# A graph-attention and a graph-mean layer, fused: straight code for the batches, features ahead of scores, and adjacency words transposed by DMA

## What is computed

```python
feats = einsum('bnf,hfu->bhnu', x, W)                   # layer 0, 8 heads
dense = leaky_relu(e_self[..., :, None] + e_neigh[..., None, :], 0.2)
dense = dense + NEG_BIG * (1.0 - adj[:, None])
out = einsum('bhij,bhju->bhiu', softmax(dense), feats) + b
x = layernorm(x + relu(out))
agg = einsum('bij,bjf->bif', adj, x) / maximum(sum(adj, -1), EPS)   # layer 1
x = layernorm(x + relu(concatenate([x, agg], 2) @ W1.T))
```

## Time and profile before

| | us |
|---|---|
| median of 3 runs | 3521.29 |
| lowest and highest run | 3521.27, 3525.59 |
| the profiled execution's own time | 3527.3 |
| its span, first to last instruction | 3525.3 |
| TensorE (PE) busy | 3383.6, 96% |
| VectorE (DVE) busy | 2466.5, 70% |
| ScalarE (ACT) busy | 1870.4, 53% |
| GpSimd (POOL) busy | 284.8, 8% |

### The profile page before, as it was taken

The page is one execution under the profiler, slowest core; times in us unless marked ns, Lnnn a source line. Parts: engine busy times, 40 slices in busy tenths (PEclk is TensorE's granted clock), DMA queues, the critical chain, the costliest instruction groups (busy, mean ns, idle before and its releaser), DMA issues.

```text
span 3525.3 us, 135227 instructions
## 1 busy us (share of the span) xinstructions
PE 3383.6 (96%) x58432; PEld 2881.7 (82%) x58432; DVE 2466.5 (70%) x4364; ACT 1870.4 (53%) x2457; POOL 284.8 (8%) x252
## 2 busy tenths in 40 slices
PE   5999999999999999999999999999999999999998
PEld 4978879787796878969789697887978879788795
DVE  4857668576685766858578585784857758577685
ACT  3736546365464645646456373563746547355463
POOL 0020200202001020010201002010020200202001
PEclk9999999999999999999999999999999999999999
DMA  4113131131321213112031221312213121131210
GB/s 170 52 43 117 39 103 56 50 99 38 103 64 55 93 35 106 64 54 93 29 113 57 67 81 32 117 50 81 68 37 119 43 97 52 44 116 39 85 34 25
DMA packets 98401, 248.46 MB, mean 70 GB/s; under 512 B 14720, under 2 KB 14720, under 8 KB 97792
## 3 DMA queue, kind: packets, MB, share of 16 engines
q1 hardware_dynamic: 97792, 239.38, 20.5%
HBM read 205.26 MB, written 34.08 MB: 68 GB/s over the span
## 4 chain that ended last, share of the span: by engine, by line
PE 85%; DVE 8%; issue 5%; ACT 1%; DMA 0%; SPq 0%; DVEq 0%; ACTq 0%; POOL 0%; POOLq 0%
PE six L887 70%; PE pair L887 10%; DVE xs L766 2%; DVE stats L771 2%; PE six L1023 2%; DVE feat L658 1%; PE pair L916 1%; PE six L916 1%; PE pair L924 1%; PE six L924 1%; DVE rs L779 0%; ACT x_parts L502 0%; DVE trl L647 0%; DVE nb L781 0%; DVE x_parts L636 0%
## 5 line engine op out<-in xcount | busy, mean ns | idle before, releaser
L887 PE MATMUL six<-rest,mask 128*128 128x65 bf16 x16384 | 1549.8, 195 | 4.2 <-issue 4.0
L887 PE MATMUL six<-x_parts,mask 128*128 128x65 bf16 x16384 | 1549.4, 192 | 1.9 <-issue 1.3
L887 PE MATMUL six<-third,mask 128*128 128x65 bf16 x16384 | 1549.3, 192 | 0.2
L887 PEld LDWEIGHTS six<-x_parts,mask 128*128 128x128 fp8e4 x16384 | 1536.0, 97 | 8.9 <-issue 7.6
L887 PEld LDWEIGHTS six<-third,mask 128*128 128x128 fp8e4 x16384 | 1536.6, 98 | 0.0
L887 PEld LDWEIGHTS six<-rest,mask 128*128 128x128 fp8e4 x16384 | 1530.7, 96 | 6.9 <-issue 5.6
L479 ACT ACTIVATE step<-s_bc,n_step 128x1024 uint16<-128x1024 f32 x1024 | 1093.5, 1137 | 382.1 <-DVE mask L716 381.8
L716 DVE TENSOR_TENSOR mask<-adj_t,step 128x1024 uint16<-128x1024 uint16 x1024 | 651.3, 685 | 22.6 <-ACT step L479 22.6
L887 PE MATMUL six<-adj_t,x_parts 128*128 128x512 fp8e4 x1536 | 388.1, 380 | 7.1 <-ACT x_parts L502 5.6
L422 POOL TENSOR_TENSOR s_bc<-feat,rden 128x512 f32<-128x512 f32 x112 | 123.9, 1111 | 2998.0 <-DVE s_bc L759 2969.2
L887 PEld LDWEIGHTS six<-adj_t,x_parts 128*128 128x128 f16 x1536 | 146.4, 98 | 184.8 <-issue 23.6
(11 more groups left out here) (124 smaller groups left out, 4954.1 us busy)
## 6 DMA issues: line engine op xcount, KB each, us to landing
s_bc<-self_scores SPq DMA_DIRECT2D x128, 512.0 KB, 3.7
adj_nat<-in_adj_dram SPq DMA_DIRECT2D x96, 512.0 KB, 3.8
xs<-in_x_dram SPq DMA_DIRECT2D x128, 256.0 KB, 2.8
out_dram<-mask SPq DMA_DIRECT2D x128, 256.0 KB, 3.3
adj_nat<-in_x_dram SPq DMA_DIRECT2D x64, 256.0 KB, 5.0
step<-in_x_dram SPq DMA_DIRECT2D x64, 256.0 KB, 3.6
mask<-in_adj_dram SPq DMA_DIRECT2D x32, 512.0 KB, 5.0
xs<-in_L_gnn_W_dram SPq DMA_DIRECT2D x1, 2048.0 KB, 11.2
```

The costliest lines, as they stand in the source:

```text
L887: return pe.matmul(o, l, r, start=start, stop=stop, skip_group_check=True)
```

## The change

- No engine has a loop over batches: `Fori` gives way to a Python loop, and 16 batches are written out (TensorE has some 55,000 rows of program in place of 7,000). The `stand` increments go.
- A batch begins with the features of tile 4, then the scores; the features of tile 5 are made in three pieces, around the transposes of the score rows and the maximum. The waits for the old batch's last sum now stand at the start of the new one, ahead of the first product that writes where this sum reads; `x_low(7)` is ahead of this sum on VectorE. The second scores have PSUM bank 5, the maximum bank 3.
- ScalarE's copy with the row sum writes an adjacency word (`adj_word`, three slots, scaled by EDGE; the sums are scaled with it, and `degc` takes this back). SP transposes each word into `adj_t` by `dma_start_transpose` (`turn_adj` on SP). TensorE's `turn_adj` and VectorE's `adj_rows` go.
- The order of loads and of the words changes: adjacency tiles 2 and 3 are the staged ones of the first round; tiles 4 to 7 are loaded when the word of the tile four earlier is made.
- `turn_x1(0)` stands after key tile 2, not 1.
- The value rows are computed as before.

```diff
+            def adj_words(b, t):
+                landed = a_in[t % 4]
+                act.wait_ge(landed.sem, landed.at(b, 16 * (t // 4 + 1)))
+                if t >= WORD_SLOTS:
+                    turned = adj_turned[t % WORD_SLOTS]
+                    act.wait_ge(turned.sem, turned.at(b, 16 * (t // WORD_SLOTS)))
+                act.activation(adj_word[:, t % WORD_SLOTS], adj_rows_at(t), ACT.Copy, scale=float(EDGE),
                                accum_out=deg_sum[:, t:t + 1]).then_inc(deg_row.sem, 1)
...
+            def turn_adj(b, t):
+                sp.wait_ge(deg_row.sem, deg_row.at(b, t + 1))
+                sp.dma_start_transpose(adj_t[:, :, col(t)],
+                                       adj_word[:, t % WORD_SLOTS, :]).then_inc(adj_turned[t % WORD_SLOTS].sem, 16)
...
                 for t in range(T):
-                    for late in {4: (3, 4), 5: (5,)}.get(t, ()):
-                        load_late_adj(b + 1, late)
+                    if t == 1:
+                        sp.wait_ge(agg_ps.sem, agg_ps.at(b, 2 * KC))
+                    for turned in {1: (0, 1), 2: (2,), 5: (3, 4), 6: (5,), 7: (6,)}.get(t, ()):
+                        turn_adj(b + 1, turned)
+                    for late in {0: (4,), 1: (5,), 2: (6,), 5: (7,)}.get(t, ()):
+                        load_adj(b + 1, late)
                     sp.wait_ge(res_ok.sem, res_ok.at(b, t + 1))
                     load_x(b + 1, t)
                     if t >= 2:
                         store_y(b, t - 2)
                 store_y(b, T - 2)
+                turn_adj(b + 1, T - 1)
                 store_y(b, T - 1)
...
-                dve.wait_ge(at_sb.sem, at_sb.at(b, T))
+                all_turned(dve, b)
...
             def batch(b, more):
 
-                pe.wait_ge(sc_f32.sem, sc_f32.at(b, 1))
-                scores(b, 1)
-                features(b, 4)
+                if b >= 1:
+                    pe.wait_ge(o_sum.sem, o_sum.at(b - 1, T - 1))
+                features(b, 4)
+                pe.wait_ge(ft_sb.sem, ft_sb.at(b, HALF))
+                scores(b, 1)
+                if b >= 1:
+                    pe.wait_ge(o_sum.sem, o_sum.at(b - 1, T))
+                    pe.wait_ge(o2_sb.sem, o2_sb.at(b - 1, T))
+                pe.wait_ge(sc_f32.sem, sc_f32.at(b, 1))
+                features(b, 5, range(0, 2))
                 pe.wait_ge(sc_f32.sem, sc_f32.at(b, 2))
...
-            with pe.Fori(0, B - 1) as b:
-                batch(b, True)
-            batch(B - 1, False)
+            for b in range(B):
+                batch(b, b + 1 < B)
```

More of the change, by code:

```diff
@@ L201, in gat_sage_kernel @@
         tail_in = [Signal(sem(f"tail_in{t}"), 16) for t in range(HALF)]
[L202 to L207, removed]
+        a_in = [Signal(sem(f"a_in{s}"), 32) for s in range(4)]
         y_stored = [sem(f"y_stored{s}") for s in range(2)]
@@ L216, in gat_sage_kernel, with all_turned @@
         xt_lo = signal("xt_lo", T)
-        at_ps = signal("at_ps", T)
-        at_sb = signal("at_sb", T)
+        adj_turned = [signal(f"adj_turned{s}", 16 * len(range(s, T, WORD_SLOTS))) for s in range(WORD_SLOTS)]
+        def all_turned(engine, b):
+            for turned in adj_turned:
+                engine.wait_ge(turned.sem, turned.at(b, turned.per_batch))
         ft_ps = signal("ft_ps", T)
@@ L281, in col @@
             return slice(c * P, (c + 1) * P)
[L283 to L288, removed]
+        N_CONST = 6
         block = ctx.enter_context(nc.Block())
@@ L382, in _ @@
                 sp.wait_ge(sums_ps.sem, sums_ps.at(b, H * GROUPS))
-                stand(sp)
-                for t in range(STAGED, T):
+                for t in (2, 3):
                     load_adj(b + 1, t)
@@ L561, in batch @@
                         act.wait_ge(rdeg_ok.sem, rdeg_ok.at(b, 1))
[L562 to L564 removed]
+                        all_turned(act, b)
+                    for row in WORDS_AT.get(t, ()) if more else ():
+                        adj_words(b + 1, row)
                 ln1_root(T - 1)
@@ L572, in _ @@
                 x_high(0, t)
-            for t in DEG_ORDER:
-                degrees(0, t)
-            with act.Fori(0, B - 1) as b:
-                batch(b, True)
-            batch(B - 1, False)
+            for t in range(T):
+                adj_words(0, t)
+            for b in range(B):
+                batch(b, b + 1 < B)
         @block.vector
@@ L877, in _ @@
                 x_low(0, t)
-            for t in range(T):
-                adj_rows(0, t)
-            with dve.Fori(0, B - 1) as b:
-                batch(b, True)
-            batch(B - 1, False)
+            for b in range(B):
+                batch(b, b + 1 < B)
         @block.tensor
@@ L1102, in _ @@
                 turn_x(0, t)
-            for t in range(T):
-                turn_adj(0, t)
-            with pe.Fori(0, B - 1) as b:
-                batch(b, True)
-            batch(B - 1, False)
+            for b in range(B):
+                batch(b, b + 1 < B)
 _INS = ["x", "adj", "L0_gnn_W", "L0_gnn_b", "L0_gnn_a_self", "L0_gnn_a_neigh", "L1_gnn_W"]
```

134 lines of the change are left out of this document (41 added, 93 removed).

## The result

The changed kernel takes **3372.4 us** (median of 4 runs, 3370.7 to 3374.4) against 3521.6 us for the kernel before on the same chip. The ratio is 0.9574, with a 95% interval from 0.9557 to 0.9591: 149 us less, 4.3%. The forecast was 3368 us in a range from 3340 to 3430. The profiled execution took 3371.0 us, with a span of 3369.2, against 3527.3, the one that the prediction's sum was made against: 156.3 us less, where the sum had 153.2.

What follows compares the result with a forecast made beforehand. TensorE's work and gaps were taken as the bound. Per batch, 6.9 us at the boundary, 2.7 from transposes and 0.7 from a wait give 10.3; 14 times this, 7.0 and 2 leave 3374.1, less 6.0: 3368 us, range 3340 to 3430.

Steps and rivals of the forecast that it cites:

- What bounded the kernel: Whole kernel: TensorE is busy 3383.6 us, 96% of the span, so its work and its few gaps, 142 us, count.
- The boundary: From a batch's last `neighbours(7)` product to the next batch's first word in the heads: 22.9 us falls to 16.0.
- The transposes: DMA transpose of an adjacency word on SP's queue: taken as 5 us to land, between 2.8 or 3.7 and 7.6.
- the packet bound: Upper limit for one DMA transpose: 64 runs of 256 bytes per engine at 118 ns a packet, 7.6 us.
- Transposes off TensorE: Tail of a batch: six adjacency transposes among the products, in three pairs of 0.45 + 0.45 us, leave TensorE: 2.7 us.
- `turn_x1(0)`: Moved one key tile later, its products cover TensorE's wait for the features' evacuation: 0.7 us a batch.
- The start: Batch 0, words and transposes through three slots: rows at about 81, 2 us of gain counted.
- (1): Overlapping DMA transposes of 6 to 10 us delay the first mask: 3417 us at 8 us each; chance 0.15.
- (2): DMA transposes run one behind another, making the kernel slower than before: about 3770 us at 10 us each; chance 0.08.
- (3): The "issue" gap at batch boundaries stays in straight code, 3 to 4 us less gained each: about 3420 us; chance 0.10.
- (4): ScalarE, waiting at words 6 and 7 for transposes, stalls TensorE, from some 9 us a transpose; chance 0.05 with the unknown.
- a late first mask: Sign that the forecast is wrong: VectorE's first mask in the heads waiting for a DMA; no size given.

## Why the prediction was right, step by step

**What bounded the kernel.** Right. TensorE's work and its few gaps were all of it, and 40 us of transposes put back cost 40 us. What the prediction left open is how the gap's two costs hang together. It took stall, tail chain and low clock as one lump, 22.9 - 16.0 us, and set the new order against it. The lump was right and its parts were not asked for: straight code alone returns stall and clock, 65 to 76 us, and the order has 22 us to give in this kernel. Together that is 87 to 98 us beside the 100 of the sum (14 x 6.9 + 3.6), and with the transposes' 40 and the wait's 12 it comes to 139 to 150 us beside the 149 measured. The order could give more, 48 us, but once TensorE's part is shorter, SP's chain ends last.

**The boundary: 16.0 us forecast, 15.8 measured in the mean of 15.** It was 22.9 before, so 7.1 us were gained, where the sum had 6.9. At the boundary shown, of 16.3 us, by its own steps, with 0 at 1102.27: store issued at 3.1 (3.3 forecast) and landed 3.2 later; `y_out(7)` done at 6.9 (7.2); score store issued at 7.3 (7.6) and landed at 10.2, 2.9 us later, the longest of the 15 (their median is 2.1 us, and the forecast had 2.3, to 9.9); broadcast 4.1 (3.7); step 1.16 (1.06); mask 0.69. TensorE's own work in it was sized at 14.5 us; it is busy 15.23. The period between boundaries is (3164.49 - 1102.27) / 10 = 206.2 us, against a forecast of 206.4.

The last row of a later boundary, from which the period is counted:

```profile
3161.74 2.75 PE six L856 x12
```

One loss was not in the forecast: behind the first word TensorE waits again, 0.7 us in the window shown, since VectorE makes masks, value parts and evacuations at that place with 98% of its time. It is part of the 16.6 us above, of which it is about half.

**The transposes: 5 us forecast, 3.3 measured** as the median of all. That of word 7, on which the term rests, has a median of 4.2 us over the 15 boundaries, and the eight of the crowded start have one of 4.4. The value taken lay between the rows for plain transfers and the packet bound, and so did the result. The greatest landing was 5.9 us, under the bound of 7.6. That bound's premise, runs of 256 bytes, holds (1056 packets for 256 KB); the mean time of a packet, which it used, was too long for them: by the difference of the two pages, (27.1% x 3369 - 20.5% x 3525) x 16 / 135,168, a packet of theirs took an estimated 23 ns, not 118. What the prediction did not price is the issue: 1.25 us of SP for a transpose, where a plain transfer takes 0.33. At the boundary neither error shows: the issue is over at 6.1, before `y_out(7)` is done, and the score store lands about when the forecast had it. That the dearer issue fell into a wait of the queue is luck; one more transpose there is paid in full.

The Trainium skill's "VectorE: DVE Perf Modes", section "The three transpose paths", with its 1309 ns for one 128x128 block, would have given an estimated 10.5 us for eight; the trace has 3.3 us for eight in one instruction, so the figure does not scale to this shape. "Advanced Engine Details and Errata", section "X-Bar Transpose (TRN2)", which has transposes as fast as regular DMAs, agrees in the landing (3.3 us beside 3.3 for a store of the same size) and not in the issue (1.25 beside 0.33 us).

**Transposes off TensorE: 2.7 us a batch.** Right, by the kernel that gives them back.

**`turn_x1(0)`: 0.7 us.** Right in the wait (10.3 us, 15 times, there and gone), and 12.0 us in the time.

**The start: 2 us of gain forecast, about 1 us lost.** This term had the wrong sign. The first step came at 82.72 (80.99 before) and the first `x` transpose in the heads at 103.1 (101.9 before). The steps' times were about as forecast (word 7 at 75.6, rows at 82.7 in place of 81). What the working left out is the 11 us in which TensorE stood almost idle, waiting for the score copy (queued on ScalarE behind the words), and after which it ran at a clock of 0.50:

```profile
65.00:76.00 11.00, 0.54 (x3) 0.11 (x1) 0.00 (x0) 4.89 (x9) 0.00 (x0) 0.74 1.13 300
76.00:80.90 4.90, 4.67 (x17) 3.56 (x18) 2.46 (x9) 0.74 (x5) 0.00 (x0) 0.50 0.45 120
```

By this term alone the forecast time was 3 us too low.

**The rivals.** (1) and (2), slow or serial transposes, fall by the 3.3 us and by the kernel with one more transpose, which costs 1.3 us a batch, its issue. (3), the gap stays, falls by the kernel before in straight code. (4), ScalarE's stalls, are there in the start alone (7.6 us). The rule of the prediction that a late first mask would be VectorE's wait for a DMA was met in another form: it waited for ScalarE's step, and that for the broadcast.

## What to carry to other kernels

A branch back in an engine's program can hold that engine for microseconds (3.3 here) and, on TensorE, cost the clock of what comes after (2.0 us here); look at whether the chain has "issue" at each turn of the loop, and price both. Work that is moved off the bound engine onto a DMA queue is paid in the queue's issue time (1.25 us for a transpose here), if a late chain runs through that queue. Before a number is read off one boundary, look at the others: the one shown here had the slowest score store of 15. Once the bound engine is packed at a boundary, follow the chain of the next one: here a store behind a load that waits for later work held back 18 us, and two lines of SP in another order gave 3352.6 us, 5.1% (4.9 to 5.2) below the kernel before.

## What the runs showed of the hardware

- A backward branch over this large body held its engine 3.3 us on TensorE and 3.15 us on VectorE; straight code showed no such wait. The longest wait for "issue" ahead of a product is 0.6 us in the kernel after and 1.3 in the kernel before in straight code. The instruction queue of the latter moved 7.60 MB, against 8.18 with loops.
- TensorE's clock after a pause: 5.0 to 5.3 us idle, it fell at 14 of 14 boundaries (12 products in 4.4 to 5.5 us). 2.0 us idle, it fell at 11 of 15 in one kernel and at 9 of 15 in the other with the same order, and stayed at 1.00 at the rest (24 products in 7.4 or 5.8 us). 1.8 us idle, it stayed at 15 of 15 in straight code and fell at the one such boundary of the kernel before. The same pause came out both ways, so from these runs no bound can be read.
- A transpose of 128 x 1024 16-bit words within SBUF by one DMA takes 1.25 us of the issuing queue (up to 2.8 in the crowded start) and lands 3.3 us after its start (2.7 to 5.9), in 1056 packets. A store of 16 KB queued behind one landed after 2.1 us in the median of 15, behind two after 2.1 too, and behind none after 1.5 to 1.8. Why it takes some tenths longer, whether by the queue or by shared engines, was not separated.
